# Leaving out the filler products on TensorE in the first two tiles of a conditioned transformer block

## The reference

```
norm(x, t)   = (t @ gw.T + gb) * x * rsqrt(mean(x*x) + eps) + (t @ bw.T + bb)   per sequence
x1           = x + attention(norm1(x, t))     16 heads of 16 channels, 64 x 64 scores each
reference    = x + x1 + swiglu(norm2(x1, t))  hidden width 1024
```

## Time and profile before

| | us |
|---|---|
| median of 3 runs | 1129.42 |
| lowest, highest | 1127.95, 1131.92 |
| span of the profiled execution | 1131.1 |
| TensorE busy, matmuls | 1094.5 (97%) |
| TensorE busy, weight loads beside them | 985.1 (87%) |
| VectorE busy | 752.0 (66%) |
| ScalarE busy | 427.2 (38%) |
| GpSimd busy | 304.8 (27%) |

### The profile page before, as it was taken

The page is one execution under the profiler, slowest core; times in us unless marked ns, Lnnn a source line. Parts: engine busy times, 40 slices in busy tenths (PEclk is TensorE's granted clock), DMA queues, the critical chain, the costliest instruction groups (busy, mean ns, idle before and its releaser), DMA issues.

```text
span 1131.1 us, 20909 instructions
## 1 busy us (share of the span) xinstructions
PE 1094.5 (97%) x7244; PEld 985.1 (87%) x7244; DVE 752.0 (66%) x1434; ACT 427.2 (38%) x887; POOL 304.8 (27%) x268
## 2 busy tenths in 40 slices
PE   5889999999999999999999999999999999999988
PEld 4778989898998989899898989989898998989876
DVE  4366667676866767686676768667676866767552
ACT  3223343433434343343434334343433434333232
POOL 4041313133231313323131332313133231323222
PEclk9679999999999999999999999999999999999999
DMA  4906244251623425162342516244251623416000
GB/s 149 213 5 126 61 85 122 48 126 31 144 60 83 121 46 124 34 144 60 83 121 46 122 36 144 60 83 121 43 121 39 142 62 83 121 42 144 2 19 19
DMA packets 37400, 97.18 MB, mean 86 GB/s; under 512 B 6784, under 2 KB 24384, under 8 KB 31104
## 3 DMA queue, kind: packets, MB, share of 16 engines
q1 hardware_dynamic: 37152, 96.76, 36.6%
q10 hardware_dynamic: 224, 0.10, 0.0%
HBM read 12.95 MB, written 8.39 MB: 19 GB/s over the span
## 4 chain that ended last, share of the span: by engine, by line
PE 90%; issue 5%; DVE 2%; POOL 1%; DMA 1%; ACT 0%; SPq 0%; POOLq 0%; DVEq 0%
PE ps L834 11%; PE ps L835 10%; PE ps L839 10%; PE ps L733 10%; PE ps L734 10%; PE ps L735 10%; PE ps L823 9%; PE ps L801 9%; PE ps L813 5%; PE ps L748 1%; PE ps L740 1%; PE ps L940 1%; DVE x_scaled L503 1%; PE ps L764 1%; DMA result<-in_modT 0%
## 5 line engine op out<-in xcount | busy, mean ns | idle before, releaser
L296 POOL TENSOR_TENSOR h_lo<-shared,h_hi 128x512 fp32r<-128x512 f32 x128 | 166.8, 1303 | 420.3 <-ACT h_hi L416 420.3
L411 ACT ACTIVATE shared<-ps 128x512 f32<-128x512 f32 x128 | 76.3, 596 | 246.7 <-PE ps L839 246.7
L733 PE MATMUL ps<-out_w_hi,h_hi 128*128 128x256 f32 x512 | 153.0, 299 | 1.4 <-POOL h_lo L296 1.4
L801 PE MATMUL ps<-k_stack,q_stack 96*128 96x64 f32 x1024 | 140.7, 283 | 5.0 <-DMA q_stack<-q_lo 5.0
L735 PE MATMUL ps<-out_w_hi,h_lo 128*128 128x256 f32 x512 | 144.3, 282 | 0.0
L734 PE MATMUL ps<-out_w_lo,h_hi 128*128 128x256 f32 x512 | 144.1, 282 | 0.0
L421 ACT ACTIVATE probsT<-ps 128x512 f32<-128x512 f32 x128 | 76.5, 598 | 172.2 <-PE ps L813 172.2
L801 PEld LDWEIGHTS ps<-k_stack,q_stack 96*128 96x128 f32 x1024 | 131.0, 200 | 5.8 <-DMA q_stack<-q_lo 5.8
L823 PEld LDWEIGHTS ps<-values,probsT 128*128 128x128 f32 x1024 | 130.5, 197 | 3.7 <-issue 1.2
L823 PE MATMUL ps<-values,probsT 128*128 128x66 f32 x1024 | 132.3, 273 | 1.3 <-DVE att L561 0.8
L569 DVE TENSOR_REDUCE row_max<-ps 128x8 f32<-128x512 f32 x128 | 87.7, 685 | 55.0 <-PE ps L801 54.3
(11 more groups left out here) (89 smaller groups left out, 2191.4 us busy)
## 6 DMA issues: line engine op xcount, KB each, us to landing
q_stack<-q_hi SPq DMA_DIRECT2D x128, 256.0 KB, 4.2
k_stack<-k_hi SPq DMA_DIRECT2D x128, 128.0 KB, 2.4
q_stack<-q_lo SPq DMA_DIRECT2D x64, 256.0 KB, 4.6
x_in<-in_x SPq DMA_DIRECT2D x16, 512.0 KB, 3.9
k_stack<-k_lo SPq DMA_DIRECT2D x64, 128.0 KB, 2.4
out<-result SPq DMA_DIRECT2D x15, 512.0 KB, 3.0
shared<-in_attT SPq DMA_DIRECT2D x1, 1024.0 KB, 6.8
shared<-in_gateT SPq DMA_DIRECT2D x1, 1024.0 KB, 8.7
```

The source lines that it names most:

```text
L296: nc.gpsimd.tensor_tensor(h_lo[:, j % 2, :], h[:, :], h_hi[:, j % 2, :].bitcast(F32), ALU.subtract).then_inc(h_lo_done, 1)
L733: nc.tensor.matmul(dst, a_hi, b_hi, start=first, stop=False, skip_group_check=skip)
L801: last = nc.tensor.matmul(ps[:, score_bank(t, p), tok], q_stack[:, r % 2, c, b, :], k_stack[:, r % 2, c, tok], start=True, stop=True)
```

## The change

The helper, its constants and its six calls are removed. All other instructions, waits and their order on each engine stay.

```diff
-FILL_K, FILL_S0, FILL_S1, FILL_STEP = 8, 10, 6, 4
 FILL = 16 * 2 * STACK
...
-            def keep_clock_up(products):
-                for n in range(products):
-                    nc.tensor.matmul(ps[:, HIDDEN, :], att_w_hi[:, 0, 0, 0:P],
-                                     att_w_hi[:, 1, :, :].rearrange("p c n -> p (c n)"), start=True, stop=True)
...
             pe.wait_ge(w_hi_done, 1)
-            keep_clock_up(FILL_K)
             pe.wait_ge(w_split, 1)
             project_k(0)
...
                     if alone(t) and p == 0:
                         pe.wait_ge(q_lo_done, CH)
-                        keep_clock_up(FILL_S0)
                         scores(t, 0)
                     if not alone(t) and attend:
                         if isinstance(t, int) and t == 1 and p == 0:
                             pe.wait_ge(q_lo_done, 2 * CH)
-                            keep_clock_up(FILL_S1)
                         scores(t, p)
-                        if isinstance(t, int) and t == 1 and p < LAG:
-                            keep_clock_up(FILL_STEP)
                     if alone(t) and p + 1 < PAIRS:
                         scores(t, p + 1)
-                        keep_clock_up(FILL_STEP)
```

## The result

The changed kernel takes 1136.01 us (median of 20 runs, 1130.5 to 1139.45), the kernel before 1129.39 (20 runs, 1125.06 to 1135.56). The ratio is 1.0054, with a 95% interval of 1.0037 to 1.0071. The change costs some 6 us; forecast were -0.4 us and a range that ends at 1133.2.

What follows compares the result with a forecast made beforehand. At the low clock TensorE was taken to bound tile 0's steps, fillers being a third of them. Terms 0 + 0.4 - 5.7 + 1.5 + 1.9 + 1.5 gave -0.4 us off the median 1129.42: 1129.0, range 1125.6 to 1133.2.

Steps and rivals of the forecast that it cites:

- the start: Ahead of tile 0, eight fillers before K removed: K starts 1.8 us earlier but runs at the low clock; +0.4 us.
- tile 1's projections: From K of tile 1 on: they begin at the low clock until dense work lifts it; +1.5 us, at most 3.0.
- its opening: Tile 1, first scores to first gate product: low clock throughout, 12.3 us and not 10.4; +1.9 us.
- its first gate products: Tile 1's gate and hidden products: low clock at their start again; +1.5 us, bounds 0.5 and 3.0.
- tile 0's seven groups: Tile 0, steps 0 to 6, four fillers each: removal brings K of tile 1 earlier; -5.7 us.
- they don't hold the clock up: Tile 0's fillers: granted clock 0.50 from 35.2 to 59.0 and 66.0 to 79.4 us although TensorE is busy.
- the 5.87 us of a step: Tile 0 step on TensorE: scores 1.71, fillers 1.85, probabilities times values 1.60, transposes 0.71 us.
- the tail: After 112 us to the end: the change touches nothing there; 0 us.
- B: Rival, chance 0.14: the clock stays down through tile 1's projections; sum +7 us, 1136.5.
- C: Rival, chance 0.08: stacking transfers, not TensorE, set tile 0's steps, which don't shrink; +2.5 us, 1131.9.
- A: Rival, chance 0.13: tile 0's gain is kept, costs behind it fall from 4.9 to some 1 us; 1125.1.

Runs made afterwards that it cites:

- xin_early_nofill: Changed kernel (no fillers) with tile 1's input loaded ahead of tile 0's second round of stacking transfers; 1.0019 of before, median 1133.17 us.
- tile0_steps_only: Kernel before with only the 28 fillers inside tile 0's steps kept; 1.0038 of before (1.0022 to 1.0053).
- before_again: The kernel before, unchanged, under another name for a second profile; 1.0002 of before, profiled span 1123.1 us.
- long_waits: Kernel before with 26 fillers, not 10, ahead of tile 0's first scores and 14, not 6, ahead of tile 1's; 0.9998 of before.
- tile1_only: Kernel before with only tile 1's 14 fillers kept (6 ahead of its first scores, 4 after each of its first two scores); 1.0018 of before.
- long_no_steps: Kernel before with 26 and 14 fillers ahead of the first scores of tiles 0 and 1, none inside tile 0's steps; 0.9987 of before.
- no_tile0_steps: Kernel before without the 28 fillers inside tile 0's steps, the other 32 kept; 1.0011 of before, median 1130.95 us.
- all_three_long: Kernel before with two GpSimd weight splits moved, tile 1's input loaded early, 26 and 14 fillers ahead of first scores; 0.9953 of before, median 1123.60 us.

## Why the prediction was wrong

**Four terms came near, the sum did not.** Between the two profiles the start (+0.4 forecast, +0.5 measured), tile 1's projections (+1.5, +1.9), its opening (+1.9, +2.1) and its first gate products (+1.5, +1.8) came nearly as worked out. In all four the stretch ran at the low clock from its start. K of tile 1, for one, ran its first nine products 0.43 us apart, then 0.24. Some luck is in the size of the opening: with its fillers it took from 9.04 to 11.85 us in nine profiles, without them 12.43 to 12.52 in four, so another profile of before would have given another cost.

**The step that failed is tile 0's seven groups, -5.7 us.** It failed twice. First, it was -3.1 between the two profiles. I had seen that the next tile's input would become late, but let it land in 6.2 us as before; it took 8.4. So the sums of squares started 16.3 us after the first scores and not 13.9, which is 2.4 of the 2.6 us missing. `xin_early_nofill` shows that with the load out of the way they start at 13.4 and K of tile 1 comes 2.9 us earlier (39.5 and 42.5). Why the load took 8.4 is not shown in full.

Second, I took "they don't hold the clock up" and the 5.87 us of a step from one execution, at a mean clock of 0.980, where the median of 94 runs is 0.985. Tile 0 in the eight profiles that have the order of GpSimd and of the loads as before:

| profile | fillers in tile 0's steps | first scores to K of tile 1, us |
|---|---|---|
| before | 28 | 45.55 |
| `tile0_steps_only` | 28 | 43.70 |
| `before_again` | 28 | 39.32 |
| `long_waits` | 28 | 38.54 |
| `tile1_only` | 0 | 42.64 |
| changed kernel | 0 | 42.45 |
| `long_no_steps` | 0 | 41.31 |
| `no_tile0_steps` | 0 | 40.84 |

Without the 28 products the stage takes 40.8 to 42.6 us. With them it takes anything from 38.5 to 45.6, and the forecast was made on the longest. The means of the two groups are equal, 41.8 us. Over many runs the 28 products cost nothing: leaving them out alone made the kernel 1.2 us slower (`no_tile0_steps`, -0.5 to 2.9), what the stages behind lose by it included. So for tile 0 this term should have been near zero.

**What the 7.0 us are made of.** Forecast were -0.4 us, and the medians are 6.6 apart. Tile 0 between the two profiles accounts for 2.6, the four other terms together for 1.0, the time ahead of the first transposes and the tail, both put at nothing, for 1.7. The remaining 1.6 are the difference between the profiled executions, 3.5 and 1.9 us above the medians of their kernels. I noted that the span of before was 1.7 us above the median, put that down to scatter, and then took a sum made on this execution off the median.

**The rivals.** B had the sign but the wrong place: the clock did not stay down through tile 1's projections (1.00 from 84.1). It stayed down for all of tile 0, where I had counted the low clock as a loss already taken. C was half right: its sign, a wait of TensorE for q_stack inside tile 0, was there (1.47 us at 51.81), but it held nothing up, and the steps shrank. What took 2.4 us of tile 0's gain was the transfer of the input. A did not occur. The tail of the profile, +1.2 us, was not foreseen: from tile 1's second gate product on, all three kernels without any filler take 1019.3 to 1019.4 us, and so does one with fillers (`all_three_long`, 1019.2), where the other nine profiles have 1017.9 to 1018.1. Whether it belongs to the change wasn't tested.

**The clock after a wait.** The Trainium skill (TensorE: Matmul & The Clock Gate, section "HAM oscillation — how this bites in real kernels") has the rule, drawn on in the prediction, that each burst behind a wait starts cold. It pointed to the right side. I set it aside for tile 0 on the strength of 13.4 busy us at 0.50. The traces bear out both readings: the fillers there don't always lift the clock, but all seven profiles that have them show it at 1.00 in part of tile 0. The six without show 0.50 from the first scores to within 2 us of K of tile 1 or beyond, apart from the first 3 us of `long_no_steps`.

## What to carry to other kernels

Before a sum is made on a profile, see where that execution stands among the runs, by time and by mean granted clock; where the clock comes out differently from one execution to the next, as here, a stage's share of low clock in one of them is a draw and not a property of the kernel. Filler products paid here behind a wait, ahead of a stretch of short steps that dense work follows (14 products for some 4 us). They have to be judged by the stage behind them, not by their own length. Where VectorE's scaling is on the path, try to keep GpSimd's long operations out of its way: here this was worth 5 us, nearly as much as all the fillers.

## What the runs showed of the hardware

- Four scalings of 128x256 on VectorE took 1.14 us alone and 5.3 to 5.4 beside GpSimd's subtraction. Ahead of tile 0 no semaphore ordered the two. VectorE started first in all nine such profiles: by 0.86 and 0.95 us in two, where the first transposes came at 10.3 and 11.0 us, and by 0.46 us or less in the other seven, where they came at 14.6 to 16.4. Since both happened in the kernel before, this is probably part of its scatter.
- A busy share of 1.00 did not say whether the clock would rise: 13.4 us of it stayed at 0.50 in the first profile of before, while in the second the clock rose right behind the fillers of step 0, with the same instructions.
- Ahead of the first record of the clock the column shows 1.00 while the products run at the low pace: eleven products of K in the changed kernel, from 21.28 to 25.55 us, were 0.43 us apart.
